# GpSimd row gathers beside the mask stage of a graph attention kernel

## The reference

```python
q, k, v = (x @ Wq + bq), (x @ Wk + bk), (x @ Wv + bv)      # (n, H, C)
alpha = einsum('ehc,ehc->eh', q[dst], k[src]) / sqrt(C)
p = exp(alpha - segment_max(alpha, dst)[dst])
out = segment_sum(p[:, :, None] * v[src], dst) / segment_sum(p, dst)
return out (heads side by side, or their mean) + x @ Ws + bs
# layer 1: H = 4, concatenated, then relu; layer 2: H = 2, mean
# result: layernorm(x + layer2(relu(layer1(x))))
```

## Time and profile before

| | us |
|---|---|
| time, median of 2 runs (2586.08 to 2586.59) | 2586.34 |
| span of the profiled execution, first to last instruction | 2580.9 |
| mask stage, from DVE's first to its last instruction of it | 139.70 to 605.65 |
| first instruction of layer 1's attention | 609.71 |

### The profile page before, as it was taken

How to read it: one execution, slowest core, us unless ns; L and a number is a source line. 1 busy time by engine, 2 the same in 40 slices (tenths; PEclk the granted TensorE clock), 3 DMA queues, 4 the chain that set the end, 5 groups by cost and what they waited for, 6 DMA issues and landing times. The chain is left out here.

```text
span 2580.9 us, 64168 instructions
## 1 busy us (share of the span) xinstructions
PE 2360.8 (91%) x18557; PEld 2004.2 (78%) x18558; DVE 2026.2 (79%) x6021; ACT 1651.1 (64%) x3383; POOL 433.0 (17%) x876
## 2 busy tenths in 40 slices
PE   2778888887999999999999999998789999999995
PEld 1356666666888888888888888888468999999995
DVE  5699999997888878888878878887237777777775
ACT  1689999995666666666666666665116665566653
POOL 4410000000211111121212111121011121211211
PEclk8889999999999999999999999999899999999998
DMA  2012222223211211112112112110312221222210
GB/s 71 1 59 87 87 86 86 86 86 93 54 31 33 55 34 36 48 34 54 30 34 54 30 34 54 33 31 9 134 42 68 63 73 48 73 60 61 73 48 26
DMA packets 46697, 141.98 MB, mean 55 GB/s; under 512 B 7621, under 2 KB 22828, under 8 KB 40249
## 3 DMA queue, kind: packets, MB, share of 16 engines
q1 hardware_dynamic: 43103, 136.94, 19.1%
q10 hardware_dynamic: 3396, 2.42, 0.4%
HBM read 91.34 MB, written 48.00 MB: 54 GB/s over the span
## 5 line engine op out<-in xcount | busy, mean ns | idle before, releaser
L1084 ACT ACTIVATE probT_l<-transposed_l 125x500 f16<-125x500 f32 (+1 forms) x1050 | 569.7, 543 | 669.5 <-PE transposed_l L1264 655.2
L1133 DVE CUSTOM_DVE_ANT_0 prob_l<-score_l,mask_l 125x500 f32<-125x500 f32 (+1 forms) x1050 | 649.8, 620 | 256.1 <-PE score_l L1239 210.6
L1239 PE MATMUL score_l<-KT,QT_l 128*125 128x500 f16 (+1 forms) x3150 | 771.1, 354 | 24.1 <-issue 17.6
L1145 DVE SCALAR_TENSOR_TENSOR probT_l<-transposed_l,probT_l 125x500 f16<-125x500 f32 (+1 forms) x1050 | 651.0, 620 | 125.4 <-ACT probT_l L1084 119.3
L1275 PE MATMUL output_l<-V,probT_l 125*125 125x256 f16 x3750 | 739.8, 275 | 0.0
L1277 PE MATMUL output_l<-V,probT_l 125*125 125x128 f16 x3750 | 680.9, 219 | 0.0
L1264 PEld LDWEIGHTS transposed_l<-ident,prob_l 125*125 125x125 f32 x3750 | 549.5, 188 | 91.8 <-DVE probT_l L1145 6.7
L1264 PE MATMUL transposed_l<-ident,prob_l 125*125 125x125 f32 x3750 | 589.5, 275 | 5.0 <-DVE probT_l L1145 5.0
L1077 ACT ACTIVATE prob_l<-prob_l,neg_max_l 125x1000 f32<-125x1000 f32 (+1 forms) x450 | 521.5, 1159 | 0.0
L1275 PEld LDWEIGHTS output_l<-V,probT_l 125*125 125x125 f16 x3750 | 512.3, 137 | 9.7 <-issue 0.2
L1277 PEld LDWEIGHTS output_l<-V,probT_l 125*125 125x125 f16 x3750 | 516.9, 138 | 0.0
(11 more groups left out here) (176 smaller groups left out, 1723.2 us busy)
## 6 DMA issues: line engine op xcount, KB each, us to landing
mask_l<-mask_scratch SPq DMA_DIRECT2D x48, 1367.2 KB
mask_scratch<-work SPq DMA_DIRECT2D x128, 273.4 KB
mask_l<-mask_scratch SPq DMA_DIRECT2D x48, 158.7 KB
hT_scratch<-rowsT_l SPq DMA_DIRECT2D x25, 250.0 KB, 2.2
hT<-hT_scratch SPq DMA_DIRECT2D x6, 1000.0 KB, 13.5
mask_scratch<-work SPq DMA_DIRECT2D x128, 31.7 KB
mask_l<-mask_scratch SPq DMA_DIRECT2D x2, 929.7 KB
xres<-in_x SPq DMA_DIRECT2D x1, 1562.5 KB
```

Source lines behind the costliest of these rows:

```text
L1084: act.activation(probT[:, p, 0, 0:b - a], flip_bank(h, p)[0:TP, 0:b - a], ACT.Copy, scale=P_UP).then_inc(s_hi, 1)
L1133: dve.tensor_tensor_reduce(out=prob[:, h % 2, a:b], in0=score_bank(h, p)[0:TP, 0:b - a], in1=mask[:, parity, a:b], scale=1.0, scalar=-3.0e ...
L1145: dve.scalar_tensor_tensor(probT[:, p, 1, 0:b - a], flip_bank(h, p)[0:TP, 0:b - a], P_UP, probT[:, p, 0, 0:b - a], ALU.mult, ALU.subtract) ...
L1239: last = pe.matmul(score_bank(h, p)[0:TP, 0:b - a], QT[:, h % 2, i, :], KT[:, h, j, a:b], start=n == 0, stop=n == len(parts) - 1)
```

## The change

SP loads, behind the loads of the edge ends, 160 source numbers for each of 125 partitions (`edge_src`). After its addition to `xres` GpSimd computes `edge_block` (a fifth of the source number, as an integer) and issues 160 indirect DMAs that each gather 125 rows of `x` of 512 B (the "near" ones, into four buffers in turn) and then 66 that each gather 125 blocks of four rows, 2 KB (the "wide" ones, into three buffers in turn). Each waits until the last gather into its buffer has landed. The buffers lie in the memory of `ends_i`. Nothing reads what is gathered. At the stream's end GpSimd waits for all of them.

```diff
@@ mask_and_projections
-        ends_i = sb("ends_i", [CP, 2, CG * CE], I32)
+        ends_all = sb("ends_i", [C, 2 * CG * CE], I32)
+        ends_i = ends_all[0:CP, :].rearrange("p (w n) -> p w n", w=2)
...
+        edge_src = sb("edge_src", [CE, 160], I32)
+        edge_block = sb("edge_block", [CE, 64], I32)
+        near = ends_all[0:CE, 0:4 * C].bitcast(F32).rearrange("e (r n) -> e r n", r=4)
+        wide = ends_all[0:CE, 4 * C:16 * C].bitcast(F32).rearrange("e (r n) -> e r n", r=3)
+        s_near, s_wide, s_esrc = [sem(f"near_gathered{i}") for i in range(4)], [sem(f"wide_gathered{i}") for i in range(3)], sem("edge_src_ready")
@@ sync
                 ends_in(sp, 1, src)
+                sp.dma_start(edge_src[:, :], src.rearrange("(p n) -> p n", p=CE)[:, 0:160]).then_inc(s_esrc, 16)
@@ gpsimd
                                    bs2_sb[:, :].unsqueeze(1).broadcast_to([TP, NT, C]), ALU.add).then_inc(s_const, 1)
-
+                pool.wait_ge(s_esrc, 16)
+                pool.tensor_scalar(edge_block[:, :], edge_src[:, 0:64], 0.2, None, ALU.mult).then_inc(s_esrc, 1)
+                pool.wait_ge(s_esrc, 17)
+                for j in range(160):
+                    wait(pool, s_near[j % 4], 16 * (j // 4))
+                    pool.indirect_dma_start(out=near[:, j % 4, :], out_offset=None, in_=x,
+                                            in_offset=bass.IndirectOffsetOnAxis(ap=edge_src[:, j:j + 1], axis=0)).then_inc(s_near[j % 4], 16)
+                x_wide = x[0:3124].rearrange("(a b) c -> a (b c)", b=4)
+                for j in range(66):
+                    wait(pool, s_wide[j % 3], 16 * (j // 3))
+                    pool.indirect_dma_start(out=wide[:, j % 3, :], out_offset=None, in_=x_wide,
+                                            in_offset=bass.IndirectOffsetOnAxis(ap=edge_block[:, j % 64:j % 64 + 1], axis=0)
+                                            ).then_inc(s_wide[j % 3], 16)
+                for i in range(4):
+                    pool.wait_ge(s_near[i], 16 * 40)
+                for i in range(3):
+                    pool.wait_ge(s_wide[i], 16 * 22)
```

## The result

The changed kernel took 2698.91 us (2681.90 and 2715.92 in two runs) against 2586.34, a ratio of 1.044 with an interval from 1.028 to 1.060: slower by more than 2%. The same kernel took 2658 to 2714 us in one later set of runs (e5) and 2618 to 2621 us in another, on another chip (e11), while the medians of the kernel before stay between 2582 and 2588 us. The profiled execution took 2681.9 us, with a span of 2679.9, 99.0 over the span of before.

What follows compares the result with a forecast made beforehand. The prediction took DVE in the mask stage as the bound. Its terms summed to 2580.9 + 0 + 0 + 79 = 2659.9 us of span, 2665 us with the 5.4 us around it; the range was 2584 to 2830 us.

Steps and rivals of the forecast that it cites:

- What bounds the kernel: Mask stage: DVE sets the pace, busy 460.28 of 464.30 us; what slows it moves the kernel's end about equally.
- The prediction's last sentence: Mask stage: prediction wrong if DVE's instructions keep their length, or PE, let down in longer waits, becomes the bound; unpriced.
- SP's load and GpSimd's tensor_scalar: Before the gathers: an 80 KB load of edge_src, taken as 0, and one tensor_scalar of 0.3 us; no cost.
- How long a gather takes: GpSimd in the mask stage: 1.1 to 1.6 us each, landing 4.6 to 4.9 us, ending well inside 470 us.
- Transfers: Mask stage: 27.1 MB beside the mask stores, DMA share from 0.28 to 0.47, covered by idle engines; cost nothing.
- What GpSimd's work does to DVE: Mask stage: gathers hold DVE's SBUF instructions, 0.44 us x 0.80 x 226 = 79 us; bounds 0 and 195.
- the sign that was set on the mean of L646: DVE in the mask stage: the mean of L646, 0.371 us before, was to be watched in the changed profile.
- A: The forecast, mask stage: DVE is delayed by each gather, 2665 us, own range 2626 to 2781; chance 0.40.
- B: Mask stage, not slower: DVE's delay hidden or small, under 0.23 us per gather; 2586 to 2615 us; chance 0.31.
- C: Mask stage: gathers wait for turns beside DVE and finish after the stage; 2736 or 2809 us; chance 0.25.
- D: Mask stage: gathers land far slower than 4.9 us and landing sets the pace, from 8.3 us on; chance 0.03.
- What would show it: Changed profile's mask stage: signs such as the distance between DVE's windows, 7.2 us before, 8.4 in A, 7.2 in C.

Runs made afterwards that it cites:

- e5: The changed kernel again with no edit, in the second set of runs: 2702.7 us (2658–2714), 1.033 of the kernel before.
- e11: The changed kernel again with no edit, in the third set, on another chip: 2619.7 us (2618–2621), 1.012 of the kernel before.
- e2: The changed kernel without its 160 near gathers, so the 66 wide ones alone from the stage's start: 2602.5 us, 1.006 of the kernel before.
- e1: The changed kernel without its 66 wide gathers, so the 160 near ones alone: 2599.4 us, 1.004 of the kernel before.
- e8: The 160 near gathers alone again, the changed kernel without its wide ones, on another chip: 2597.3 us, 1.004 of the kernel before.
- e4: The changed kernel with 276 GpSimd iotas in place of the 226 gathers, no DMA: 2630.1 us, 1.017 of the kernel before.
- e7: The changed kernel with the two loops exchanged, wide gathers first, then near ones: 2707.2 us (2623–2720), no ratio given.
- e6: The changed kernel with the last 66 gathers reading rows of 512 B instead of 2 KB: 2728.2 us, 1.057 of the kernel before.

## Why the prediction was right, and which of its terms were not

The direction held, the time lies in the range, and 2665 stands 34 us under 2699. But the sum came about by other terms than its own, and that it came so near is luck: the price of DVE's delay was some five times too high, and slow windows, which had no price, stood in for it. Where they stayed out, the same kernel took 2620 us, 1.2% over before.

- **What bounds the kernel.** Right for the kernel before, and for the changed kernel without slow windows (DVE 140.00 of 140). In the measured result it is wrong for ten windows: there DVE is busy for 87.60 of 140, and the chain through PE, at its lower clock, and ACT sets the pace. The prediction's last sentence names this, PE let down in longer waits, as what would make it wrong. It had no chance and no price there, and it was worth 73.6 of the 99.0 us, so by its own sign the account failed where the number held. How much of the 73.6 is DVE held by gathers inside the slow windows, where its 224 instructions take 0.39 us each against 0.31 before (140.00 / 448), no run separates from the waits.
- **SP's load and GpSimd's tensor_scalar.** The latter took 0.81 us, not 0.3. The near and the wide gathers alone, each measured with the load, leave 4 to 7 of e11's 32.1 us open, and nothing points to the load.
- **How long a gather takes.** Right: 1.21 us, 1.51 from issue to issue, 1.87 beside a full DVE (140 / 75); 1.1 to 1.6 was taken. Landing was under-sized for the wide ones: 154 / 66 = 2.33 us each with three buffers, so some 7.0 us from one gather to the next into its buffer, not 4.9. All the same the gathers ended far inside the stage.
- **Transfers, costed at nothing.** Mis-sized: 15.4 us (e2), 16.5 in the profile after. The cover named, the idle part of the DMA engines, is an average; stores landed late enough beside the wide gathers that ACT waited for them (13.5 us in e2). The share that it forecast, 0.47, was 0.69 while the wide gathers ran.
- **What GpSimd's work does to DVE.** This term failed in its size: 79 us, 0.35 for each gather, against 0.06 to 0.08 (e1, e8), so some 16 us for 226 of them. A hold exists (19 col_hot of 0.7 us), but the rows it was priced by the earlier trace rows are elementwise instructions, and even an iota hands on only a quarter of its length (e4). Beside a DVE without a gap it is mostly the gather that waits. The 0.44 us was also misread: it is the mean of two delays by one L500, so that these rows give 0.87 us for one GpSimd instruction. And the sign that was set on the mean of L646 can't tell A from B, since behind the last gather, in windows of 7.2 us, it is 406 ns in the profile after and 372 in e5.
- **The rivals.** On e11's chip B is what happened: 0.14 us for each gather in sum (32.1 / 226), under its limit of 0.23, and 2620 us beside its 2586 to 2615. A's own range, 2626 to 2781, doesn't hold that time. C fell: gathers are done before the stage ends (at 558 of 705 us), and there is no stretch of GpSimd alone. D fell too. The Trainium skill, SBUF — State Buffer, "Who interferes with whom", says that of a GpSimd instruction and a VectorE instruction in a two-port mode the one that starts first blocks the other for the whole instruction. The runs agree in that either side is held (2.5 against 1.21 us, 0.7 against 0.4), but not in the length: a held col_hot loses 0.36 us, not the 1.21 of a gather; and whether these DVE instructions are of the two-port kind no run shows. The 3100 against 620 ns that the same page of the Trainium skill gives (section "A bandwidth-pool intuition that's wrong (but worth ruling out)") isn't there: beside DVE without a gap a near gather takes 1.56 us on average (L528 of e11). The outer range's 2584 is called B's low end, where B's own times start at 2586.
- **What would show it.** Windows of 8.4 us were to show A. In truth there were 14.6 us on average, then 7.6, then 8.1: three regimes, and only the view by stretches tells them apart from one mean.

**Settled:** the near gathers' price at PE's full clock, what the wide gathers cost alone, with ACT's waits for the mask stores beside them, and that the rest is slow windows. Windows of 11 to 16 us were seen only beside gathers of 512 B, and ended at the latest one window behind the last of them; in the profile after they ended at 300 us while near gathers went on to 404. **Open:** why they set in. The changed kernel has them in the result and in e5 and not in e11, and on e5's chip one of e7's four runs, 2623 us, stands where no slow windows would put it, so the chip alone doesn't decide. In e7 the waits came before the lower clock, but what tips the stage into that state, and why it can hold while near gathers run, no run tells. Near gathers alone, a late start and the slower pace weren't tried on a chip that had them.

## What to carry to other kernels

This stage, in which three engines are all 87 to 100% busy, has two ways to run: in step, or, once the head start is gone, in turns, with PE at its lower clock much of the time, and then the loss is many times the disturbance. Other stages weren't tried. So price an added stream twice, by what it takes from the engine that sets the pace and by what happens if the engines fall out of step, and give the second a chance. Cost transfers by who waits for the ones already there, not by the average idle share of the DMA engines; and repeat the kernel on several chips before a single difference is explained.

## What had not been expected of the hardware

- An indirect DMA of 125 rows occupies GpSimd for 1.21 us, for rows of 512 B and of 2 KB alike; what differs is the landing (through three buffers, short rows followed each other at 1.55 us in e6, wide ones at 2.33).
- Beside a DVE without a gap (e11) a gather and a DVE instruction hold each other in a fixed pattern: four gathers to one window, one of them 2.5 us long, and windows of 7.2, 7.5 or 7.9 us.
- The same program took 2658 to 2714 us in six runs on one chip and 2618 to 2621 in four on another, while the kernel before differs by 6 us between them.
